# Six products with one adjacency matrix on one core: from one pass per product to sweeps in which a split tile serves two products

## What is computed

```
u = x
for _ in range(3):
    v = mlp(adj @ u, uv_W1, uv_b1, uv_W2, uv_b2, uv_W3, uv_b3)
    u = mlp(adj @ v, vu_W1, vu_b1, vu_W2, vu_b2, vu_W3, vu_b3)   # the third u is never used
x = layernorm(x + v)
x = layernorm(x + adj @ (x @ gcn_W))
```

## Time and profile before

| | us |
|---|---|
| median of 3 runs | 1229.32 |
| lowest, highest | 1228.20, 1230.36 |
| profiled execution, device time | 1229.88 |
| its span (first to last instruction) | 1227.9 |
| PE busy | 1206.0 |
| DVE busy | 1005.8 |
| ACT busy | 873.1 |

### The profile page before, as it was taken

How to read it: one execution, slowest core, us unless ns; L and a number is a source line. 1 busy time by engine, 2 the same in 40 slices (tenths; PEclk the granted TensorE clock), 3 DMA queues, 4 the chain that set the end, 5 groups by cost and what they waited for, 6 DMA issues and landing times.

```text
span 1227.9 us, 13400 instructions
## 1 busy us (share of the span) xinstructions
PE 1206.0 (98%) x5376; PEld 969.5 (79%) x5376; DVE 1005.8 (82%) x624; ACT 873.1 (71%) x690; POOL 11.0 (1%) x29
## 2 busy tenths in 40 slices
PE   6999999999999999999999999999999999999997
PEld 5788778877887788778877887787778787788886
DVE  4888888888888888888888888888888888787884
ACT  4777777777777777777777777777777777677773
POOL 2000000000000000000000000000000000000000
PEclk9999999999999999999999999999999999999999
DMA  8899998798889798989878899978888886799992
GB/s 344 319 359 346 352 341 341 273 352 341 340 340 351 274 341 340 352 342 340 334 292 339 341 341 351 342 271 324 303 322 311 314 323 238 287 371 345 365 362 88
DMA packets 56365, 397.69 MB, mean 324 GB/s; under 512 B 6544, under 2 KB 6672, under 8 KB 8432
## 3 DMA queue, kind: packets, MB, share of 16 engines
q1 hardware_dynamic: 55440, 394.88, 85.2%
q0 software_dynamic: 864, 1.97, 0.4%
HBM read 394.73 MB, written 2.10 MB: 323 GB/s over the span
## 4 chain that ended last, share of the span: by engine, by line
PE 96%; ACT 1%; DMA 1%; DVE 1%; issue 0%; SPq 0%; ACTq 0%; DVEq 0%
PE acc L530 85%; PE layer L473 6%; PE proj L479 3%; DMA raw<-adj_dram 1%; PE minus_mean L491 1%; PE var L497 1%; ACT high L223 1%; PE spread L511 1%; DVE low L350 1%; ACT squared L257 0%; SPq L151 0%; DVE p_low L383 0%; ACT p_high L266 0%; SPq L157 0%; DVE h L371 0%
## 5 line engine op out<-in xcount | busy, mean ns | idle before, releaser
L350 DVE TENSOR_TENSOR low<-raw,high 128x2048 fp32r<-128x2048 f32 x372 | 846.9, 2292 | 182.6 <-ACT high L223 181.8
L223 ACT ACTIVATE high<-raw 128x2048 fp32r<-128x2048 f32 x372 | 712.2, 1915 | 84.2 <-PE acc L530 75.9
L530 PE MATMUL acc<-high,p_low 128*128 128x512 f32 x1536 | 644.3, 419 | 9.0 <-DVE low L350 6.9
L530 PE MATMUL acc<-low,p_high 128*128 128x512 f32 x1536 | 601.2, 391 | 0.0
L530 PE MATMUL acc<-high,p_high 128*128 128x512 f32 x1536 | 600.8, 391 | 0.0
L530 PEld LDWEIGHTS acc<-high,p_low 128*128 128x128 f32 x1536 | 289.4, 188 | 89.1 <-issue 30.6
L530 PEld LDWEIGHTS acc<-high,p_high 128*128 128x128 f32 x1536 | 289.5, 188 | 79.1 <-issue 22.8
L530 PEld LDWEIGHTS acc<-low,p_high 128*128 128x128 f32 x1536 | 289.0, 188 | 62.0
L238 ACT ACTIVATE z<-layer,b_uv_b 128x512 f32<-128x512 f32 x48 | 33.1, 690 | 70.1 <-PE layer L473 70.1
L355 DVE SCALAR_TENSOR_TENSOR h<-z 128x512 f32<-128x512 f32 x120 | 82.7, 689 | 0.0
L227 ACT ACTIVATE p_high<-proj 128x512 fp32r<-128x512 f32 x40 | 23.9, 599 | 69.0 <-PE proj L479 69.0
(11 more groups left out here) (45 smaller groups left out, 259.2 us busy)
## 6 DMA issues: line engine op xcount, KB each, us to landing
raw<-adj_dram SPq DMA_DIRECT2D x372, 1024.0 KB, 5.2
resid<-x_t_dram SPq DMA_DIRECT2D x8, 256.0 KB, 15.7
kept<-adj_dram SPq DMA_DIRECT2D x2, 1024.0 KB, 16.3
out_t_dram<-z POOLq DMA_DIRECT2D x3, 256.0 KB, 5.3
out_t_dram<-normed POOLq DMA_DIRECT2D x3, 256.0 KB, 5.4
out_t_dram<-z SPq DMA_DIRECT2D x1, 256.0 KB, 2.1
out_t_dram<-normed SPq DMA_DIRECT2D x1, 256.0 KB, 2.0
w_vu_W<-vu_W_dram POOLq DMA_DIRECT2D x3, 64.0 KB, 6.8
```

What stands on the lines that cost most here:

```text
L223: nc.scalar.activation(high[slot][:], source[:], ACT.Copy).then_inc(high_ready, 1)
L350: nc.vector.tensor_tensor(low[slot][:], source[:], high[slot][:].bitcast(F32), ALU.subtract).then_inc(low_ready, 1)
L530: done = nc.tensor.matmul(acc[side][:], part[parity][:, at:at + D], adj_part[slot][:, columns], start=(g == 0 and j == 0 and i == 0), stop ...
```

## The change

**Order.** The matrix is now handled in tiles of 128 x 1024 (512 KB, `PER_TILE = 2` blocks). A use of a tile for one product is a *visit*: 6 matmuls. There are 768 visits, numbered by the order on PE, and 496 tile loads, since 272 tiles are visited twice, once for product k and once for product k+1. For that a chunk's sum is broken up: the part of product k+1 whose p exists already is summed while product k runs, and put aside in SBUF (`part`, ACT, "keep"); blocks whose p came late are added later (`grow`, DVE, "more"), and the last piece is added to it (`finish`, DVE, into `total`). Products go alternately from chunk 0 up and from 7 down, so that the tiles next to the diagonal (`corner`) come first. Each transition from one product to the next has about 22 tiles with one visit each. Product 5 has nobody after it: its last 72 visits (696 to 767) have one fresh tile each. In the 6 visits before these, tiles held back from chunk 7 (`HELD`) are visited the second time. Four PSUM banks are used for sums instead of two.

**Queues.** There are 5 raw slots of 512 KB (before: 4 of 1 MB and 2 kept) and 8 slots for high and low (4 of twice the size). The position of each tail operation is a number of visits after the chunk's `start`; a tile's split stands 6 visits ahead of its first visit (`AHEAD`), on ACT and DVE.

**Tails.** Bias and leaky ReLU are one ACT operation (`Prelu`); DVE's leaky ReLU is gone. The layer norms have no centring and no variance matmul: PE transposes the sum (4 blocks of 128), DVE takes `bn_stats` and `bn_aggr` of the 4 blocks, ACT the root, DVE the inverse and the shift, and ACT writes the result with 4 operations of 128 columns (`normalize`). For product 5 the transposed sum first gets x added (DVE, into `scaled`), and each turn waits for the `normalize` of the chunk before. The dense layers are matmuls in plain fp32 as before.

The core of the diff:

```diff
+PER_TILE = 2
+TILE = PER_TILE * CHUNK
+TILES = N // (PER_TILE * D)
+IN_BAND = TILES // CHUNKS
+PRODUCTS = 6
+NORMED = PRODUCTS - 2
+LAST = PRODUCTS - 1
+RAWS = 5
+SLOTS = 8
+AHEAD = 6
+BANKS = 4
+HELD = 6
...
-LAYER_2_AT, LAYER_3_AT, PROJECT_AT = 1, 3, 5
-NORM_LAYER_2_AT, NORM_LAYER_3_AT, NORM_CENTER_AT, NORM_VAR_AT, NORM_PROJECT_AT, NORM_SPREAD_AT = 1, 2, 4, 5, 6, 6
-LAST_CENTER_AT, LAST_VAR_AT, LAST_SPREAD_AT = 1, 2, 5
+LAYER_2, LAYER_3, PROJECT, P_LOWER = 3, 6, 8, 9
+ADD_X, TURN, ROOT, SCALE, NORMALIZE, NORM_P_LOWER = 7, 9, 10, 11, 12, 12
+SPACING = [2] * NORMED + [4, 3]
+BETWEEN = 12
+LAST_TURN, LAST_MEASURE, LAST_ROOT, LAST_SCALE = 2, 2, 3, 4
...
+    def both(self, chunk, columns, first, second, held):
+        kept = []
+        for i, column in enumerate(columns):
+            t = self.tile(chunk, column)
+            self.visit(t, first)
+            if i < len(columns) - held:
+                self.visit(t, second)
+            else:
+                kept.append(t)
+        for t in kept:
+            self.visit(t, second)
...
+    def sweep(self, k):
+        rows = list(range(CHUNKS)) if k % 2 == 0 else list(range(CHUNKS))[::-1]
+        def corner(r, goal):
+            self.one(rows[r], self.band([rows[r]]), self.open(k, rows[r], goal))
+        for r in (1, 2, 3):
+            corner(r, "more")
+        corner(0, "finish")
+        self.one(rows[1], self.band(rows[:1]), self.open(k, rows[1], "finish"))
+        for r in (4, 5, 6):
+            corner(r, "more")
+        made = self.one(rows[2], self.band(rows[:2]), self.open(k, rows[2], "finish"))
+        self.one(rows[1], self.band(rows[:1]), self.open(k + 1, rows[1], "keep"))
+        second = self.open(k + 1, rows[2], "keep")
+        for t in made:
+            self.visit(t, second)
+        for r in range(3, CHUNKS - 1):
+            first = self.open(k, rows[r], "finish")
+            self.both(rows[r], self.band(rows[:r]), first, self.open(k + 1, rows[r], "keep"), 0)
+        first = self.open(k, rows[-1], "whole")
+        self.one(rows[-1], self.band(rows[-1:]), first)
+        self.both(rows[-1], self.band(rows[:-1]), first, self.open(k + 1, rows[-1], "keep"), HELD)
...
+    def last_sweep(self):
+        rows = list(range(CHUNKS))[::-1]
+        for r in range(1, CHUNKS - 1):
+            self.one(rows[r], self.band([rows[r]]), self.open(LAST, rows[r], "more"))
+        self.one(rows[0], self.band(rows[:1]), self.open(LAST, rows[0], "finish"))
+        for r in range(1, CHUNKS - 1):
+            self.one(rows[r], self.band(rows[:r]), self.open(LAST, rows[r], "finish"))
+        self.one(rows[-1], self.band(rows), self.open(LAST, rows[-1], "whole"))
...
+        def split_before(t):
+            return max(0, plan.opening[t] - AHEAD, plan.closing[t - SLOTS] + 1 if t >= SLOTS else 0)
...
+            def rectify(source, bias, i):
+                return nc.scalar.activation(h[i % 2][:], source, ACT.Prelu, bias=bias, alpha=SLOPE)
...
+            def normalize(i):
+                act.wait_ge(shift_ready, i - NORM + 1)
+                c = sums[chunks[i].total].chunk
+                if i >= FINAL + 2:
+                    act.wait_ge(out_stored[i % 2], 16 * ((i - FINAL) // 2))
...
+                    target = block_in(h[i % 2], j) if i >= FINAL else resid[:, bass.ds(c * CHUNK + j * D, D)]
+                    source = scaled if i >= FINAL else flip
+                    done = nc.scalar.activation(target, block_in(source, j), ACT.Identity,
+                                                bias=shift[:, j:j + 1], scale=rstd[:, j:j + 1])
+                done.then_inc(normed_ready, 1)
...
+            def grow(s):
+                kept_before(s)
+                dve.wait_ge(visited, s.closes + 1)
+                nc.vector.tensor_tensor(part[:, blocks_of(s.chunk)], acc[sums.index(s) % BANKS][:],
+                                        part[:, blocks_of(s.chunk)], ALU.add).then_inc(part_grown, 1)
...
+            def finish(i):
+                s = sums[chunks[i].total]
+                kept_before(s)
+                dve.wait_ge(visited, s.closes + 1)
+                if 0 < i <= FINAL:
+                    dve.wait_ge(first_ready, i)
+                if i > FINAL:
+                    dve.wait_ge(turned, i - NORM)
+                nc.vector.tensor_tensor(total[:], acc[chunks[i].total % BANKS][:], part[:, blocks_of(s.chunk)],
+                                        ALU.add).then_inc(total_ready, 1)
...
+            def measure(i, source):
+                for j in range(IN_CHUNK):
+                    nc.vector.bn_stats(stats[:, j, :], block_in(source, j)).then_inc(stats_ready, 1)
+                for j in range(IN_CHUNK):
+                    dve.wait_ge(stats_ready, (i - NORM) * IN_CHUNK + j + 1)
+                    done = nc.vector.bn_aggr(moments[:, j, :], stats[:, j, :])
+                done.then_inc(moments_ready, 1)
...
+            def measure_sum(i):
+                dve.wait_ge(turned, i - NORM + 1)
+                dve.wait_ge(normed_ready, i - NORM)
+                nc.vector.tensor_tensor(scaled[:], flip[:], resid[:, blocks_of(sums[chunks[i].total].chunk)],
+                                        ALU.add).then_inc(turned_added, 1)
+                dve.wait_ge(turned_added, i - FINAL + 1)
+                measure(i, scaled)
...
+            def invert(i):
+                dve.wait_ge(std_ready, i - NORM + 1)
                 nc.vector.reciprocal(rstd[:], std[:]).then_inc(rstd_ready, 1)
+                dve.wait_ge(rstd_ready, i - NORM + 1)
+                nc.vector.scalar_tensor_tensor(out=shift[:], in0=moments[:, :, 0], scalar=-1.0, in1=rstd[:],
+                                               op0=ALU.mult, op1=ALU.mult).then_inc(shift_ready, 1)
...
+            def scale_projected(i):
+                dve.wait_ge(proj_done, CHUNKS + i + 1)
+                nc.vector.tensor_tensor(
+                    scaled[:].rearrange("p (j d) -> p j d", d=D), proj[:].rearrange("p (j d) -> p j d", d=D),
+                    rstd[:].unsqueeze(2).to_broadcast([D, IN_CHUNK, D]), ALU.mult).then_inc(scaled_ready, 1)
...
+            def turn(source, i):
+                if i > NORM:
+                    pe.wait_ge(normed_ready, i - NORM)
+                for j in range(IN_CHUNK):
+                    done = nc.tensor.transpose(block_in(flip, j), block_in(source, j), identity[:])
+                done.then_inc(turned, 1)
...
+            def turn_total(i):
+                if finishes(i):
+                    pe.wait_ge(total_ready, sums[chunks[i].total].nth + 1)
+                else:
+                    pe.wait_ge(taken, 1)
+                turn(total, i)
```

More of the change, by code:

```diff
@@ L132, in kept_of, with way_of @@
-        def kept_of(chunk, g):
-            return kept[g - GROUPS + KEPT] if (isinstance(chunk, int) and chunk == 0
-                                               and GROUPS - KEPT <= g < GROUPS) else None
-        def split_ahead(split, product, chunk, first, last):
-            for g in range(first + LEAD, last + LEAD):
-                split((product * CHUNKS + chunk) * GROUPS + g, g % SLOTS,
-                      loads_of(product, chunk, g), kept_of(chunk, g))
+        def way_of(i):
+            return "uv" if sums[chunks[i].total].product % 2 == 0 else "vu"
@@ new lines, in finishes, with layered, plain, normed @@
+        def finishes(i):
+            return sums[chunks[i].total].goal == "finish"
+        def layered(i):
+            return i < FINAL
+        def plain(i):
+            return i < NORM
+        def normed(i):
+            return NORM <= i < FINAL
+        def split_before(t):
+            return max(0, plan.opening[t] - AHEAD, plan.closing[t - SLOTS] + 1 if t >= SLOTS else 0)
+        split_at = [split_before(t) for t in range(len(tiles))]
+        def made_by(product, chunk):
+            if product == 0:
+                return chunk + 1
+            return CHUNKS + 1 + next(i for i, c in enumerate(chunks) if sums[c.total].product == product - 1
+                                     and sums[c.total].chunk == chunk)
@@ L143, in gnn_kernel, with over_with @@
+        def over_with(product, chunk):
+            return 1 + max(n for n, v in enumerate(visits) if sums[v.total].product == product
+                           and v.column // IN_BAND == chunk)
         block = ctx.enter_context(nc.Block())
@@ new lines, in _ @@
+            load_x(0)
+            load(0)
+            load_x(1)
+            for t in range(1, RAWS):
+                load(t)
+                if t % IN_BAND == 0:
+                    load_x(t // IN_BAND + 1)
+            for t in range(RAWS, len(tiles)):
+                if t % IN_BAND == 0 and t // IN_BAND + 1 < CHUNKS:
+                    load_x(t // IN_BAND + 1)
+                load(t)
+            for i in (len(chunks) - 2, len(chunks) - 1):
+                sp.wait_ge(normed_ready, i - NORM + 1)
+                sp.dma_start(out_t[sums[chunks[i].total].chunk], h[i % 2][:]).then_inc(last_stored[i % 2], 16)
```

(17 more changed lines are left out.)

763 lines of the change are left out of this document (350 added, 413 removed).

## The result

| | before | after |
|---|---|---|
| median, us | 1228.76 (1227.73 to 1230.36) | 1236.55 (1234.42 to 1237.64) |
| profiled execution: time, span | 1229.9, 1227.9 | 1237.0, 1235.2 |
| ratio, 95% interval | | 1.006 [1.0042, 1.0078] |

A forecast was written before the change was run, and what follows sets the result against it. PE was taken to bound the kernel: 1191.7 us of span without waits, plus 3.0 transitions, 3.0 into product 4, 30.4 waiting in product 5 and 1.9 slow clock gave 1230.0, 1232.0 of device time; 8 in 10 range 1208 to 1247.

The forecast's parts named there:

- The start: Up to visit 16: it would begin at 43.7 us, a gain of 3, bounds 0 and 5.
- Three transitions: Transitions 0-1, 1-2 and 2-3: small waits between ACT, DVE and PE of 1.0 us each, together 3.0, bounds 0 and 5.
- Into product 4: The way into product 4: the turn waits for DVE's `add_x`, which stands behind splits, 3.0 us.
- the 4.0 gap before product 5: The old wait for p's late low part and slow clock, 4.0 us; gone, since p is made 6 visits before use.
- Product 5: From visit 690: 143.2 us against PE's own 112.8, so 30.4 of waiting (bounds 20 and 38), plus 1.9 for slow clock.
- the term for the hand-off: Product 5, per chunk: DVE idle 2.65 us while ACT does four `normalize` (1.6) and then the next split (0.95 to 1.05).
- The tail: After the last matmul: 9.1 us instead of 10.1.
- Rival 1: DVE and ACT pass work without a stop, hiding the 2.65 us; seven cycles give back 2.9 each: 1212 us; chance 0.20.
- Rival 3: Slower supply: three of five raw slots in flight, deciding from about 1.5 us a tile; 1244 or 1266 us; chance 0.15.
- Rival 4: Slower transitions: three hand-offs each behind splits, 1.5 us each and 1.9 for the clock, +20: 1252 us; chance 0.08.
- rival 2: All hidden: every wait is taken up by the six visits of lead, 1194 us; chance 0.07.
- The rule on transfer size: The skill's 1 MiB per DMA rule would put a tile above 1.54 us and the sum some 5 us higher.

The follow-up runs named there:

- x2: The changed kernel with seven buffers for raw tiles instead of five; 1229.3 us, ratio 1.0006 to the kernel before.
- x5: The changed kernel with seven raw buffers and, in product 5, `normalize` one position later, behind ACT's split; 1221.4 us, ratio 0.9926.
- x9: x5 with DVE taking product 5's statistics of one block of 128 columns, not four; 1218.5 us, ratio 0.9925.
- x10: x5 with product 5's sums taken long and short by turns, each in one piece, without six additions on DVE; 1220.0 us, ratio 0.9932.
- x4: The changed kernel with the last pieces of product 4 starting three visits apart instead of four; 1237.9 us, ratio 1.0068.
- x7: The changed kernel with chunk 34 started two visits later, so DVE measures chunk 33 ahead of its sum for chunk 34; 1236.6 us, ratio 1.0049.
- x1: The changed kernel with product 5's `normalize` on ACT one position later, behind its split instead of ahead; 1228.2 us, ratio 0.999.
- x12: x3 with the last product 4 chunk's p ahead of a split (1203.4 us), plus product 5's kept buffers joining the raw ones, six in a ring; 1197.7 us, ratio 0.9747.
- x3: The kernel before, its visit order and tiles kept, with the change's dense layers, Prelu and layer norm by statistics; 1206.0 us, ratio 0.9806.

## Why the prediction was right, and where not

Forecast 1232.0, range 1208 to 1247, slower the likelier sign; measured 1236.55, inside the forecast's own 1222 to 1240. Span for span 1230.0 was forecast and 1235.2 came. By its own steps:

- **The start** (43.7): 45.2, the gain 1.5 and not 3; other profiles of the same start had 43.9 to 45.0. Visit 4 began at 24.9, not 22.4. I had let eight tiles stream in at 350 GB/s. But a tile needs a free buffer: the chain has three splits on DVE until 15.28, then a load of 6.52, which landed at 21.81, not 19.5. Still, two more buffers aren't shown to help: in x2, x5, x9 and x10 that load was issued some 2.5 us earlier, took 8.1 to 9.6 us and landed at 20.4 to 21.4, and with five buffers it landed at 20.5 to 21.8.
- **Two-visit stretches**: free, as forecast; 0.2267 per matmul stood.
- **Three transitions** (1.0 each): 1.24, 1.25, 1.27.
- **Into product 4** (3.0): 7.9. This is the step that failed. Its words were that the turn waits for `add_x`; it does, for 1.4 us. But "the 4.0 gap before product 5 has no successor" looked only at the last chunk's p, which has six visits of lead. Chunk 33's p is wanted by visit 592, in the position in which it is made. The chain:

```profile
924.77 0.80 DVE stats L538 x4
925.57 0.29 DVE moments L541 x4
...
926.67 0.96 ACT high L371
...
927.64 1.23 DVE low L490
...
929.15 0.61 DVE scaled L565
929.79 0.64 ACT p_high L429
930.45 0.70 DVE p_low L572
...
931.20 5.49 PE acc L693 x12
```

2.6 us idle, and 12 matmuls in 5.49 instead of 2.72, since the clock had dropped (granted 0.50 of full speed there), as in the earlier trace rows. With the 1.4 at the turn that is 6.8 of the 7.9; the rest is small stops. x4 and x7 show that neither of the two neighbours tried is to blame; what the chain shows is that one chunk's way (8 us) is longer than its three visits. That a plan with more visits between would remove the wait wasn't tested.
- **Product 5** (143.2 from visit 690, of it 30.4 waiting, or 145.1 with 1.9 for the clock): 144.1. The walk of the queues held, to within 0.3 us for the first three turns and 2.3 for the rest. The turns could begin, by the forecast, at 37.7, 47.1, 56.5, 69.3, 84.6, 102.7, 123.6; they began at 37.9, 47.4, 56.2, 68.5, 83.3, 100.4, 122.9. Of the 31 us above PE's own 112.8 it stood idle for 21; the rest is mostly slow clock, which the forecast had within its waits. x1 confirms the term for the hand-off: 1.6 of the 2.65 was `normalize`, and moving it gave 6.9 us. Only its last steps rest on another cause than I gave them: the cycles of 10 and 12 visits had 0.5 and 1.0 for late tiles, and x2 puts 4.8 us on buffers. Too much for DVE (the cycles of 6 and 8 visits took 12.4 and 14.8, not 12.8 and 15.3) and too little for supply cancelled, so that the total came out within 1 us is in part luck.
- **The rates.** Splits of 1.22 and 1.05 were right to 0.01, `bn_stats` and `bn_aggr` took 0.87 and 0.29 for four of each, 1.16 instead of 1.48. The busy sums were taken too high, 694 and 643 instead of 730 and 690; 266 MB instead of 262.
- **The tail** (9.1): 8.2.

The sum of the differences is 1.5 + 0.8 + 4.9 - 1.0 - 0.9, or 5.3 us; the span shows 5.2.

**The rivals.** None came true whole. Rival 1 (no stop between the engines) is what x1 builds, and gave 7 of its 20 us, since not all of the hand-off is `normalize`. Rival 3 named the mechanism of x2 and x12, and a threshold of 1.5 us a tile; the real figure, 7.4 to 7.7 us over five buffers, sits right on it; it was at work in the last cycles, for some 5 us and not 12. Rival 4 (transitions) has its price at product 4 alone, and rival 2 (all hidden) fell.

**The rule on transfer size.** The same stretch near the start, first in the changed kernel, then in x2, all of it loads of 512 KB, and below a stretch of the kernel before with loads of 1 MB beside x's of 256 KB:

```profile
28.00:40.00 12.00, 12.00 (x71) 10.49 (x70) 11.23 (x11) 8.84 (x12) 0.00 (x0) 1.00 0.96 351
```

```profile
28.00:40.00 12.00, 12.00 (x68) 10.36 (x67) 10.91 (x12) 9.16 (x13) 0.00 (x0) 1.00 1.03 409
```

```profile
20.00:28.00 8.00, 5.80 (x33) 4.91 (x32) 5.88 (x4) 4.15 (x5) 0.00 (x0) 1.00 1.03 418
```

With seven buffers loads of half a megabyte ran at 409 GB/s, above the 373 of the earlier trace rows and the 387 of x12, and 2% under the fastest of these stretches with 1 MB. The Trainium skill ("DMA: Bandwidth & Descriptors", rules for kernel authors) asks for at least 1 MiB per DMA. The measurement decides: half the size cost no more than 2% of the rate here, and what counted was how many loads could be under way. More buffers don't help without limit: from 28 to 40 us the median load took 7.4 us with seven buffers and 4.7 with five.

**What the change did.** PE gained in the layer norms what the sum said: x3's chunks take 24.96 and 22.25 where the earlier trace rows have 26.82 and 24.10, 1.86 and 1.85 less (2.34 less 0.49 was forecast). The pair sweeps spare DVE a quarter of its work (x3 939 us, the changed kernel 694), but ACT, DVE and DMA didn't bound the kernel; and they leave all eight last norms to 78 visits, 72 of which want a fresh tile. With the order of before, the new tails alone take 22 us off, 1.9%.

## What to carry to other kernels

A streamed tile's period is (load + every engine's pass over it) / number of buffers; put it beside the consumer's pace ahead of any reading of GB/s. Twice here (7.5 / 5 against 1.36, and 11.7 to 12.4 / 4 against 2.78) it was just over, and two more buffers freed it; the second time 363 GB/s at a DMA share of 0.96 had looked like bandwidth used up. Take the load's duration with the new number under way, since it grows when the queues fill. When engines work in program order, walk one chunk's whole chain through their queues and compare it with the visits that the plan gives it, for every product: a saving spread over the program is worth nothing if the last stretch gathers all the tails, and the place of `normalize`, 1.6 us a chunk, ahead of a split was worth 7 us.

## What the runs showed of the hardware

The same wait doesn't always cost the same clock. x2 waited as long at visit 592 as the changed kernel (2.62 us idle against 2.63), and its next 12 matmuls took 3.03 us where the other's took 5.49:

```profile
930.15 3.03 PE acc L693 x12
```

The granted clock is the last figure but two, for the changed kernel and then for x2:

```profile
931.20:936.70 5.50, 5.50 (x13) 4.34 (x14) 1.23 (x1) 2.14 (x5) 0.00 (x0) 0.50 0.27 85
```

```profile
930.15:933.20 3.05, 3.05 (x13) 2.54 (x14) 0.88 (x1) 2.14 (x5) 0.00 (x0) 1.00 0.17 70
```

So the clock was at its lower level, 1.2 GHz, in one and at 2.4 GHz in the other. Of the six profiles with the same order of work there (these two, x1, x5, x9 and x10) it stayed up in x2 and x5 alone; x9 and x10, which have seven buffers as well, saw it drop. It was worth up to 2.9 us a time. What decides it stays open.
